# Local attention: the mix of a tile's eight heads in one run, at the end of a step's first half

## The reference, cut to what matters

```python
qkv = shift_token(x) @ wqkv
q, k, v = jnp.split(qkv, 3, axis=-1)
q = l2norm(q) * qs
k = l2norm(k) * ksc
q, k = rotary_xpos(q, k)
sim = jnp.einsum('bhwid,bhwjd->bhwij', bq, bk)      # own window and the one before
sim = jnp.where(mask, -jnp.finfo(sim.dtype).max, sim)
attn = jax.nn.softmax(sim, axis=-1)
out = jnp.einsum('bhwij,bhwjd->bhwid', attn, bv)
x = x + o @ wo
```

## Time and profile before

| | |
|---|---|
| median of 3 runs | 2978.23 us (2978.09 to 2978.67) |
| the profiled execution | 2979.38 us |
| its span in the profile | 2977.6 us |
| TensorE matmuls busy | 2950.0 us (99%) |
| VectorE, ScalarE, GpSimd busy | 1617.4, 1228.9, 1156.4 us |
| transfers | 189.47 MB, mean 64 GB/s |

### The profile page before, as it was taken

The page is one execution under the profiler, slowest core; times in us unless marked ns, Lnnn a source line. Parts: engine busy times, 40 slices in busy tenths (PEclk is TensorE's granted clock), DMA queues, the critical chain, the costliest instruction groups (busy, mean ns, idle before and its releaser), DMA issues. The chain is left out here.

```text
span 2977.6 us, 44278 instructions
## 1 busy us (share of the span) xinstructions
PE 2950.0 (99%) x17048; PEld 2415.8 (81%) x17048; DVE 1617.4 (54%) x3363; ACT 1228.9 (41%) x2498; POOL 1156.4 (39%) x1194
## 2 busy tenths in 40 slices
PE   8999999999999999999999999999999999999999
PEld 7887888888878888888887888888878888888887
DVE  7976777766764333333325667776775333333331
ACT  6865555555553111111124555555565211111111
POOL 7866566655631110111113566656651111221111
PEclk9999999999999999999999999999999999999999
DMA  7741111111051011100121111111123111111110
GB/s 230 245 164 49 44 51 44 54 43 54 26 156 41 22 45 45 45 31 21 39 95 60 44 33 54 58 47 33 54 91 101 58 45 40 45 59 54 47 52 25
DMA packets 143797, 189.47 MB, mean 64 GB/s; under 512 B 21462, under 2 KB 75226, under 8 KB 143588
## 3 DMA queue, kind: packets, MB, share of 16 engines
q1 hardware_dynamic: 143588, 186.66, 19.7%
HBM read 131.39 MB, written 52.46 MB: 62 GB/s over the span
## 5 line engine op out<-in xcount | busy, mean ns | idle before, releaser
L1016 PE MATMUL quad<-fhT_f,w_h_f 128*128 128x512 f32 (+1 forms) x1392 | 551.0, 396 | 1.5 <-ACT w_h_f L1080 1.5
L1018 PE MATMUL quad<-fhT_f,w_l_f 128*128 128x512 f32 (+1 forms) x1392 | 544.9, 391 | 0.0
L1017 PE MATMUL quad<-fhT_f,w_h_f 128*128 128x512 f32 (+1 forms) x1392 | 543.4, 390 | 0.0
L1704 DVE SCALAR_TENSOR_TENSOR u_f<-quad,bias_f,gate_f_raw 128x512 f32<-128x512 f32 (+1 forms) x174 | 130.4, 750 | 699.0 <-PE quad L1018 615.8
L1773 POOL TENSOR_SCALAR stats<-stats 128x1 f32<-128x1 f32 x64 | 43.4, 678 | 1019.2 <-DVE stats L1679 1018.6
L1239 ACT ACTIVATE lprob<-lprob,small 128x384 f32<-128x384 f32 (+2 forms) x512 | 288.6, 565 | 160.5 <-DVE small L1547 160.5
L1868 POOL TENSOR_TENSOR turned_qk<-with_cos,with_sin 128x256 f32<-128x256 f32 x252 | 180.8, 738 | 444.2 <-DVE with_sin L1571 387.3
L1344 ACT ACTIVATE gate_f_raw<-quad,bias_f 128x512 f32<-128x512 f32 (+1 forms) x174 | 119.6, 687 | 507.3 <-PE quad L1018 507.3
L1080 ACT ACTIVATE uT_f<-u_f 128x512 fp32r<-128x512 f32 (+2 forms) x176 | 117.3, 667 | 510.4 <-DVE u_f L1704 510.4
L780 PE MATMUL bank_pair<-wqkv_h,hT 128*128 128x512 f32 x992 | 318.9, 402 | 0.1
L1018 PEld LDWEIGHTS quad<-fhT_f,w_l_f 128*128 128x128 f32 (+1 forms) x1392 | 256.8, 184 | 63.0
(11 more groups left out here) (227 smaller groups left out, 6044.8 us busy)
## 6 DMA issues: line engine op xcount, KB each, us to landing
s_in<-stream SPq DMA_DIRECT2D x128, 128.0 KB, 2.7
s_res<-stream SPq DMA_DIRECT2D x64, 256.0 KB, 2.9
stream<-a_out SPq DMA_DIRECT2D x64, 256.0 KB, 2.0
w_h_f_raw<-in_L_ffn_w SPq DMA_DIRECT2D x60, 256.0 KB, 5.3
h_in_f<-stream SPq DMA_DIRECT2D x112, 128.0 KB, 2.7
res_f<-stream SPq DMA_DIRECT2D x47, 256.0 KB, 3.5
x_in<-in_x SPq DMA_DIRECT2D x32, 256.0 KB, 2.9
ctx_in<-in_ctx SPq DMA_DIRECT2D x32, 256.0 KB, 2.8
```

Of the source, the lines that this page charges most:

```text
L1016: e.matmul(bank[0:n, :], high, hT[:, 0, c, :], start=c == 0, stop=False)
L1017: e.matmul(bank[0:n, :], high, hT[:, 1, c, :], start=False, stop=False)
L1018: ins = e.matmul(bank[0:n, :], low, hT[:, 0, c, :], start=False, stop=c == KC - 1)
L1704: e.scalar_tensor_tensor(out=Fm.u[q % 2][0:n, :], in0=up_bank(2 * (g * HC + j) + 1)[0:n, :], scalar=Fm.bias1[0:n, 0, j:j + 1], in1=Fm.gate ...
```

## The change

The mix of both halves of a tile is made in one run at the end of the first half of a step (tiles 0 to 29 of a layer; tiles 30 and 31 keep the old places). In step s this is tile s - 3, eight heads, 48 matmuls; the second half has no mix. For this the turned probabilities get four buffers instead of two, and the space comes from the values, of which five tiles are kept in a ring instead of eight. The copy of the values moves from the end of ScalarE's first half to its second half, behind `split_out`, since the tile that it overwrites has just been mixed. The projection is cut at 18 instead of 20.

```diff
--- before.py
+++ after.py
@@ -37,6 +37,7 @@
 WIN = 3 * P
 FREE_BASE = 16512
 SUM_AHEAD = 4
+V_TILES = 5
 WEIGHTS_AT = 5
 NORMALISE_AT = 12
 SBUF_END = 229344
@@ -130,7 +131,7 @@
 
 
 PARTS = (2, 0, 1)
-PROJECTED = ((0, 12, 20), (20, 30, 36))
+PROJECTED = ((0, 12, 18), (18, 30, 36))
 
 
 def last_summed(s):
@@ -140,6 +141,11 @@
 def sums_at(s):
 
     return range(last_summed(s - 1) + 1, last_summed(s) + 1) if s > 0 else ()
+
+
+def mixed_whole(t):
+
+    return t < TILES - 2
 
 
 def early_tile(s):
@@ -230,11 +236,11 @@
         A, sfx = Mem(), f"_{l}"
         plan = Plan(nc, at_late)
         A.kT = plan.tensor("kT" + sfx, [P, 2, PAIRS, SEQ], F32R)
-        A.v_rows = plan.tensor("v_rows" + sfx, [P, TPB, HEADS * HD])
+        A.v_rows = plan.tensor("v_rows" + sfx, [P, V_TILES, HEADS * HD])
         A.qT = plan.ring("qT", 2, [P, 2, DIM], F32R, sfx)
         A.far = plan.tensor("far" + sfx, [P, WIN])
         A.prob = plan.ring("lprob", PAIRS, [P, 2, WIN], F32, sfx)
-        A.probT = plan.ring("lprobT", 2, [P, 2, WIN], F32, sfx)
+        A.probT = plan.ring("lprobT", PAIRS, [P, 2, WIN], F32, sfx)
         A.oT = plan.tensor("oT" + sfx, [P, 2, DIM], F32R)
         assert plan.at <= at_gain
         plan = Plan(nc, at_early)
@@ -891,7 +897,7 @@
             def mix(t, d):
 
                 n = base + t
-                k, tiles, _, _ = reach(t)
+                tiles = reach(t)[1]
                 w.wait_ge(S("v_rows"), n + 1)
                 w.wait_ge(S("oT_low"), n)
                 if t == 0 and d == 0:
@@ -902,8 +908,8 @@
                         for i, half in enumerate(half_of):
                             h = 2 * p + i
                             ins = e.matmul(banks[5][half, p * P:(p + 1) * P],
-                                           A.v_rows[:, k - tiles + 1 + j, h * HD:(h + 1) * HD],
-                                           A.probT[p % 2][:, i, j * P:(j + 1) * P], start=j == 0, stop=j == tiles - 1)
+                                           A.v_rows[:, (t - tiles + 1 + j) % V_TILES, h * HD:(h + 1) * HD],
+                                           A.probT[p][:, i, j * P:(j + 1) * P], start=j == 0, stop=j == tiles - 1)
                     ins.then_inc(S("lmix"), 1)
 
             def project_out(t, half):
@@ -975,7 +981,9 @@
                         turn_early(l, 3)
                     if inside and d:
                         project(l, s, PROJECTED[1][1], PROJECTED[1][2])
-                    if mixing:
+                    if mixing and d == 0 and mixed_whole(t - 1):
+                        mix(t - 1, 0)
+                    if mixing and (d == 0 or not mixed_whole(t)):
                         mix(*turned)
                     if (s, d) == (TILES + 2, 0):
                         up(l, 0, 1, 0)
@@ -1257,9 +1265,9 @@
                 w.wait_ge(S("v_projected"), n + 1)
                 if t == 0:
                     wait_phase()
-                if t >= TPB:
-                    w.wait_ge(S("lmix"), PAIRS * (n - 5))
-                copy(A.v_rows[:, t % TPB, :], banks[0]).then_inc(S("v_rows"), 1)
+                if t >= V_TILES:
+                    w.wait_ge(S("lmix"), PAIRS * (n - 2))
+                copy(A.v_rows[:, t % V_TILES, :], banks[0]).then_inc(S("v_rows"), 1)
 
             def split_out(t):
                 n = base + t
@@ -1272,9 +1280,9 @@
                 U = 2 * n + d
                 for i, p in enumerate(duo(d)):
                     w.wait_ge(S("lprobT_turned"), 2 * U + i + 1)
-                    w.wait_ge(S("lmix"), 2 * (U - 1) + i + 1)
+                    w.wait_ge(S("lmix"), 2 * (U - 2) + i + 1)
                     at = pair_banks(p)
-                    copy(A.probT[p % 2][:, :, 0:cols], quad[:, at:at + 2, 0:cols]).then_inc(S("lprobT"), 1)
+                    copy(A.probT[p][:, :, 0:cols], quad[:, at:at + 2, 0:cols]).then_inc(S("lprobT"), 1)
 
             for s in range(TILES + 3):
                 t, tail = s - 2, s - 3
@@ -1287,6 +1295,8 @@
                         square(l, rotated_tile(s))
                     if d and ended:
                         split_out(tail)
+                    if d and 3 <= s < TILES:
+                        keep_v(s)
                     if live:
                         for h in range(4 * d, 4 * d + 4):
                             probabilities(t, h)
@@ -1295,7 +1305,7 @@
                     if (s, d) == (TILES, 1):
                         split_normalised(l, 0, early_bank(0))
                         split_normalised(l, 1, early_bank(1))
-                    if d == 0 and s < TILES and s != 1:
+                    if d == 0 and s in (0, 2):
                         keep_v(s)
                     if l and (s, d) == (0, 0):
                         e.activation(small[:, 0, 0:16], half_power[:, :], ACT.Exp).then_inc(S("table"), 1)
```

## The result

The changed kernel takes **2988.93 us** (median of 6 runs, 2988.26 to 2990.27), against 2978.45 us for the kernel before in the same runs (2977.97 to 2979.21). The ratio is 1.0036, with a 95% interval of 1.0026 to 1.0046: 10.5 us slower. The prediction had 2991 us and a range of 2984.5 to 2997.

The account below looks back on a forecast made before the run. TensorE, busy 2950.0 of 2977.6 us, was taken to bound the kernel. Terms of -9.0 + 25.4 - 3.5 = +12.9 us on the median 2978.23 gave 2991 us, range 2984.5 to 2997 (chance 0.78).

Parts of the forecast that it names:

- One mix run instead of two: At the end of each step, joining the two mix runs saves 0.15 us, 60 times: 9.0 us saved.
- The lost cover of the keys: First half's scores follow the projection and wait for kT, 0.36 us in 48 of 60 starts: 25.4 us more.
- More cover for hT: Second half's scores behind a narrow mix wait less for hT, 0.44 us at eight places: 3.5 us saved.
- the cut at 18: Two projection matmuls move from ahead of the turned h to the second half: no work more or less.
- twice was foreseen: Sign in TensorE's waits: hT named twice instead of ten times.
- the 20.99 predicted: Sign in the timeline: steady steps of 20.99 us instead of 20.78.
- The values in the second half, the ring: ScalarE's 0.60 us value copy hides in 1.23 us free behind oT's split; ring and values trade the same bytes: nothing.
- the faster rival: At the first half's scores, kT is ready 0.36 us earlier, only savings stand: 2965.7 us, chance 0.07.
- the half cover: Scores start 0.10 us behind kT, early steps lose half: 2984.4 us, or 2983; chance 0.07 with a time within 0.2%.
- The values cost nothing: Rival: ScalarE's second-half value copy delays exponentials and transposed probabilities, 3027 us, partly 2997; chance 0.08 for 2997 and above.
- a joined run that costs as much as two: Rival at the mix: the 9.0 us fall away, 3000 us; chance within the 0.08 of the values rival.
- The tiling mode: Skill's drain rule: one of six mode changes a step left out, alone making the kernel faster; rows show 0.15 us.

Follow-up runs that it names:

- the version without waits: Changed kernel with queries and keys turned between the two halves of the output projection, projection cut at 30: 2964.67 us, ratio 0.9954.
- the cut at 20: Changed kernel with the first half's projection cut at 20 instead of 18: 2987.16 us, ratio 1.0027.
- the buffers alone: Changed kernel's ring of five, four buffers and moved value copy, but mix in two runs and projection cut at 20 and 30 as before: 2978.76 us, ratio 0.9999.
- the cut at 28: Changed kernel with the second half's projection cut at 28 instead of 30, eight matmuls behind the turned keys instead of six: 2972.76 us, ratio 0.9979.
- the cut at 26: Changed kernel with the second half's projection cut at 26 instead of 30, ten matmuls behind the turned keys: 2980.25 us, ratio 1.0005.

## Why the prediction was right

The direction and the cause held. The size held in part by luck: the terms of the sum make 12.8 us by measurement and 12.9 by prediction only because two of them were too high by nearly the same amount and stand with opposite signs, the cover of the keys (2.8 us) and the cover for hT (2.7 us). By its own steps:

- **One mix run instead of two.** Predicted 9.0 us saved, 0.15 a step; the sums between the traces give 9.0, and the step of the version without waits is 20.63 us, 0.15 under 20.78. The run of 48 took 2.77 us, as said. The 0.15 us lie at two places: from the last mix matmul to the scores 0.20 us start to start, where the pairs within a run follow at 0.10, and in the run's first pair 0.15 instead of 0.10.
- **The lost cover of the keys.** Predicted 25.4 us. Measured 23.5, less the 0.9 of old waits: 22.6. The term that was mis-sized is the delay from the end of the subtraction to the scores. I took 0.15 us "for the same list of waits"; all sixty starts show 0.10, my lower bound. 60 x 0.045 = 2.7 us is the whole difference. The 0.66 us more in early-row steps (gaps of 1.29 against 0.63), and that GpSimd's part of them goes, came as worked out.
- **More cover for hT.** Predicted 3.5 us, measured 0.8. This step failed in two ways. At tile 0 the turning of h stands *ahead* of the projection's second part, so the cut at 18 took two matmuls of cover away; I had said that the cut costs no more and no less. The start of such a second half after the change:

```profile
233.21 0.55 PE L871 MATMUL quad<-kT,qT 64*128 64x128 f32 x6
233.78 0.68 DVE L1407 TENSOR_TENSOR hT<-quad,hT 128x512 fp32r<-128x512 f32 x1
...
234.52 0.55 PE L871 MATMUL quad<-kT,qT 64*128 64x128 f32 x6 [0.76 <-DVE hT L1407]
```

  The odd pairs start 1.31 us behind the even ones, 0.83 before (234.28 against 233.45). Twice 0.45 us lost. And of the eight places behind a narrow mix only five gained, 0.32 to 0.37 us each; at the other three VectorE's own list sets when hT is ready (in the second half that starts at 573.84, ScalarE's copy of hT has ended at 573.52, and VectorE comes to the subtraction only at 574.15, straight from the products with the rotation tables). The view names hT five times with 3.0 us, where twice was foreseen.
- **Other waits.** Not foreseen: the turned keys of tile 1 wait less for GpSimd (1.5 to 0.6 us), and the turned probabilities less for the maxima, since the second half's first part is longer (the cut at 20 takes 0.8 us of that back). In the table that is 3.3 us less. The 1.3 us more in the output projection weren't foreseen either; they are why a step reads 20.97 us, close to the 20.99 predicted, though the wait for kT is 0.05 us shorter than predicted.
- **The values in the second half, the ring.** Predicted free; the buffers alone make 2978.76 us against 2979.0.
- **Rivals.** The keys' cover was not kept. That it would be enough to give it back was shown by the version of 2964.67 us, 1.0 us from the faster rival's 2965.7; that it is so near is partly luck, since the rival's number holds the 3.5 us for hT. Of the half cover one part was right, the 0.10 us; the early-row steps lost all that was reckoned (0.66 us more than an ordinary step). The values cost nothing, as the buffers alone show, and a joined run that costs as much as two is refuted by the 9.0 us.
- **The tiling mode.** The rule of the Trainium skill, "TensorEngine Tiling (Array Packing)", Key Properties, is that a change of the tiling mode drains TensorE. The trace agrees in so far as one such change less saves 0.15 us a step; that a drain makes these 0.15 us, no run shows. By that rule alone the change would have been faster, and the path to the keys decided otherwise.

So +12.9 us was -9.0 + 25.4 - 3.5, and +10.9 between the traces is -9.0 + 22.6 - 0.8, less about 2 in the smaller rows.

## What to carry to other kernels

Work that looks like the thing to be merged may be the cover of a chain that nobody waits for yet: before taking it from its place, look up what becomes ready in its shadow and by how much. Here the merge was good for 13 us once the chain's start (turning the keys) had been moved ahead of other work, and bad for 10 us without. And a cover should be taken from work that nothing else leans on: the last two matmuls taken from ahead of the maxima's reader gave 3.3 us and cost nearly 13, six of the output projection cost nothing.

## What was not expected of the hardware

- The scores start 0.10 us behind the end of the subtraction for kT when a projection stands ahead of them, and 0.15 us when mix matmuls do (562.33 and 562.48 in the earlier trace rows), with the same waits in both. In the changed kernel sixty starts behind a projection show the one; the start behind 24 mix matmuls in its timeline shows the other (843.54 + 0.68 = 844.22, and 844.36, with rounded ends). What makes the difference wasn't tried.

```profile
843.54 0.68 DVE L1407 TENSOR_TENSOR kT<-quad,kT 128x512 fp32r<-128x512 f32 x1
...
844.36 0.93 PE L871 MATMUL quad<-kT,qT 64*128 64x384 f32 x7 [0.36 <-DVE kT L1407]
```

- In the cut at 28 the scores start 0.33 us behind the last projection matmul instead of 0.32, and the run itself takes 1.27 instead of 1.25 us, though nothing waits. VectorE's residual sum runs beside it there, but it does so in the changed kernel too (625.00 beside 625.18), where the run takes 1.25. An ordinary step is 20.70 us and not 20.63; 0.03 of that are the 0.03 us in the output projection that the changed kernel has as well. Why stays open.
- A wait that is nearly over when TensorE comes to it is entered as "issue", or not at all where its rows overlap (the 12.5 us of the cut at 26). The start-to-start times show it.
